# A fused Perceiver layer on one core: the cross-attention scores as plain fp32 matmuls in two column halves, and the order of three engines around them

## What is computed

```python
q = query @ Wq.T + bq;  k = mem_state @ Wk.T + bk;  v = mem_state @ Wv.T + bv
scores = jnp.einsum('btd,bsd->bts', q, k) * scale
vals, idx = jax.lax.top_k(scores, 32)          # all others are -inf
attn = jax.nn.softmax(masked, axis=-1)
x1 = x + jnp.einsum('bts,bsd->btd', attn, v) @ Wo.T + bo
```

## Time and profile before

| | us |
|---|---|
| median of 3 runs (lowest, highest) | 459.78 (457.98, 460.98) |
| the profiled execution | 461.32 |
| its span in the trace | 459.5 |
| TensorE busy | 439.7 (96%) |
| VectorE busy | 299.3 (65%) |
| ScalarE busy | 215.7 (47%) |
| GpSimd busy | 127.2 (28%) |

### The profile page before, as it was taken

The page is one execution under the profiler, slowest core; times in us unless marked ns, Lnnn a source line. Parts: engine busy times, 40 slices in busy tenths (PEclk is TensorE's granted clock), DMA queues, the critical chain, the costliest instruction groups (busy, mean ns, idle before and its releaser), DMA issues.

```text
span 459.5 us, 5828 instructions
## 1 busy us (share of the span) xinstructions
PE 439.7 (96%) x2045; PEld 325.5 (71%) x2045; DVE 299.3 (65%) x591; ACT 215.7 (47%) x321; POOL 127.2 (28%) x195
## 2 busy tenths in 40 slices
PE   6999999799999999898999999999999999999996
PEld 2587766356567656576888888887788888888884
DVE  3898787688999999968997443646862333522224
ACT  1797764354566454384877446434542111111111
POOL 3501013032222330200003272324236643333330
PEclk9999999799999999999999999999999999999999
DMA  6999924044224314103951700000000000200002
GB/s 207 412 391 386 366 98 180 2 183 183 74 112 183 139 45 184 35 11 141 396 198 38 168 1 23 1 0 1 1 1 1 1 0 1 86 7 0 1 0 92
DMA packets 26845, 49.98 MB, mean 109 GB/s; under 512 B 6208, under 2 KB 6208, under 8 KB 25792
## 3 DMA queue, kind: packets, MB, share of 16 engines
q1 hardware_dynamic: 26816, 49.61, 30.2%
HBM read 47.49 MB, written 2.11 MB: 108 GB/s over the span
## 4 chain that ended last, share of the span: by engine, by line
PE 71%; DVE 13%; ACT 6%; DMA 5%; issue 3%; SPq 1%; POOL 0%; DVEq 0%; ACTq 0%
PE bank L1237 8%; PE bank L1239 8%; PE bank L1238 8%; PE bank L1447 7%; PE bank L1678 7%; PE bank L1676 6%; PE bank L1662 6%; PE bank L1663 6%; PE bank L1418 5%; PE bank L1344 3%; DMA wab<-w1T 2%; PE bank L1244 2%; DVE mt_lo L1026 2%; PE bank L1432 2%; DVE work L1039 2%
## 5 line engine op out<-in xcount | busy, mean ns | idle before, releaser
L792 ACT ACTIVATE g<-bank,b1c 128x512 f32<-128x512 f32 x32 | 22.0, 688 | 92.0 <-PE bank L1678 92.0
L1217 DVE CAST g_hi<-g 128x512 fp32r<-128x512 f32 x32 | 13.9, 436 | 74.7 <-ACT g L792 74.6
L594 ACT ACTIVATE mt_hi<-bank 128x512 fp32r<-128x512 f32 x64 | 38.0, 600 | 49.4 <-PE bank L1418 49.4
L1026 DVE TENSOR_TENSOR mt_lo<-bank,mt_hi 128x512 fp32r<-128x512 f32 x64 | 43.1, 684 | 18.1 <-ACT mt_hi L594 17.9
L1676 PE MATMUL bank<-xt_lo,w1s 128*128 128x512 f32 x128 | 50.8, 397 | 0.0
L1678 PE MATMUL bank<-xt_hi,w1s 128*128 128x512 f32 x128 | 50.7, 396 | 0.0
L1662 PE MATMUL bank<-w2s,g_lo 128*128 128x512 f32 x128 | 50.3, 393 | 0.2 <-DVE g_lo L1219 0.2
L1663 PE MATMUL bank<-w2s,g_hi 128*128 128x512 f32 x128 | 50.0, 390 | 0.0
L487 POOL TENSOR_SCALAR w2s<-w2t 128x512 fp32r<-128x512 int8 x32 | 19.8, 620 | 65.9 <-PE bank L1663 65.9
L445 POOL TENSOR_SCALAR qs<-qT 128x256 fp32r<-128x256 f32 x16 | 6.5, 405 | 112.8 <-PE bank L1433 93.5
L1432 PE MATMUL bank<-mt_lo,qs 128*128 128x512 f32 x64 | 30.6, 479 | 0.3 <-DVE mt_lo L1026 0.3
(11 more groups left out here) (244 smaller groups left out, 1101.0 us busy)
## 6 DMA issues: line engine op xcount, KB each, us to landing
ctxr<-ctx SPq DMA_DIRECT2D x8, 1024.0 KB, 8.5
ctx<-ctx SPq DMA_DIRECT2D x8, 1024.0 KB, 7.7
wab<-w1T SPq DMA_DIRECT2D x4, 1024.0 KB, 11.4
wab<-w2T SPq DMA_DIRECT2D x4, 1024.0 KB, 8.5
wgraw<-wgT SPq DMA_DIRECT2D x4, 1024.0 KB, 6.5
wst<-w1T SPq DMA_DIRECT2D x4, 1024.0 KB, 6.2
wst<-w2T SPq DMA_DIRECT2D x4, 1024.0 KB, 6.6
resid<-x SPq DMA_DIRECT2D x4, 512.0 KB, 6.8
```

What stands on the lines that cost most here:

```text
L594: act.activation(mt_hi[:, g % 4, :], ctx_bank(g)[:, :], ACT.Copy).then_inc(mt_hi_ok, 1)
L1026: dve.tensor_tensor(mt_lo[:, g % 4, :], ctx_bank(g)[:, :], f(mt_hi[:, g % 4, :]), ALU.subtract).then_inc(mt_lo_ok, 1)
```

## The change

Scores are plain fp32 matmuls like `weigh`: step `s` of four per pair takes chunk `d` of both batches, one in each column half, with `qT` itself as weights (64 columns) and the copied chunk `mt` as the moving operand; no split of context or queries is made. Chunks alternate between the two batches and always turn over two PSUM banks. One ScalarE activation with the bias `ctok` brings a pair's scores to `s_t` (`scores_part`). `wvo` is made wholly in iterations 0 and 1 in banks 6 and 7. `project(i - 2)` runs whole at the end of iteration `i`, so the statistics and the layer-norm turn of a pair come an iteration sooner, and the ninth iteration is gone. The tail is ordered anew on all engines; the weights' slots in `wgraw`, and where the split parts lie, change with it. `wst` has three slots instead of four, and `bias_o` is loaded earlier. GpSimd adds `bias_x` to all token tiles at once and then only does `rstd`.

The core of the diff; the lines removed from the old loops, which stand above, are left out, those of the tail are shown:

```diff
--- before.py
+++ after.py
...
-                if k < 4:
-                    sp.wait_ge(wg_lo_ok[w_slot(k)], DC)
+                if k < 3:
+                    sp.wait_ge(wg_lo_ok[k + 1], DC)
                 else:
-                    sp.wait_ge(tern_ok, k - 3)
+                    sp.wait_ge(tern_ok, k - 2)
...
+            def mt_part(g):
+
+                act.wait_ge(ctx_turned, g + 1)
+                if g >= 4:
+                    act.wait_ge(scored, g // 2 - 1)
+                act.activation(mt[:, g % 4, :], bank[g % 2][:, :], ACT.Copy).then_inc(mt_ok, 1)
+
+            def scores_part(p):
+
+                act.wait_ge(scored, DC * (p + 1))
+                if p:
+                    act.wait_ge(exp_ok, p)
+                    act.wait_ge(topk, 8 * p - 6)
+                else:
+                    act.wait_ge(ctok_ok, 1)
+                act.activation(s_t[:, :], bank[2 + p % 2][:, :], ACT.Identity, bias=ctok[:, p:p + 1],
+                               scale=1.0).then_inc(scores_ok, 1)
+
...
+            for i in range(NT):
+                g = 2 * DC * i
+                mt_part(g)
+                if i >= 1:
+                    scores_part(i - 1)
+                if i == 1:
+                    wvo_hi_part(1)
+                mt_part(g + 1)
                 if i == 2:
                     wvo_hi_part(3)
+                if i >= 1:
+                    keep_exp(i - 1)
+                mt_part(g + 2)
+                if i >= 3:
+                    ln2_apply(i - 3)
+                mt_part(g + 3)
                 if i == 0:
                     abs_part(7)
+                if i >= 2:
+                    am_part(i - 2)
+                mt_part(g + 4)
+                if i < 2:
+                    wvo_hi_part(2 * i)
+                mt_part(g + 5)
+                if i >= 3:
+                    xt_part(NT + i - 3, i - 3, ln2_bank(i - 3))
+                if i >= 2:
+                    amt_hi_part(i - 2)
+                mt_part(g + 6)
                 if i == NT - 1:
+                    split_hi(0, wk_hi, 0, DC // 2)
+                mt_part(g + 7)
+                if i == NT - 1:
+                    split_hi(0, wk_hi, DC // 2, DC)
+                if i >= 1:
+                    at_part(i - 1)
+
+            scores_part(7)
+            keep_exp(7)
             ln2_apply(5)
-            split_hi(1, wv_hi, 0, DC)
-            xt_part(NT + 4, 4, ln2_bank(4))
+            am_part(6)
             xt_part(NT + 5, 5, ln2_bank(5))
-            act.wait_ge(mt_used, 4 * B)
+            amt_hi_part(6)
+            split_hi(1, wv_hi, 0, DC // 2)
+            at_part(7)
+            split_hi(1, wv_hi, DC // 2, DC)
+            ln2_apply(6)
+            am_part(7)
+            amt_hi_part(7)
+            xt_part(NT + 6, 6, ln2_bank(6))
+            act.wait_ge(scored, DC * NT)
             split_hi(2, wgq_hi, 0, DC)
-            ln2_apply(6)
-            act.wait_ge(qs_ok, 4 * NT)
+            ln2_apply(7)
+            xt_part(NT + 7, 7, ln2_bank(7))
             split_hi(3, wgg_hi, 0, DC)
-            ln2_apply(7)
-            xt_part(NT + 6, 6, ln2_bank(6))
-            xt_part(NT + 7, 7, ln2_bank(7))
 
...
+            for i in range(NT):
+                if i >= 3:
+                    add_att(i - 3)
+                    ln2_stats(i - 3)
+                if i == 0:
+                    wvo_lo_part(0)
                 if i == 1:
+                    wvo_lo_part(1)
                     scales()
                 if i == 2:
                     wvo_lo_part(3)
+                if i >= 1:
+                    top8(i - 1, 0)
+                    top8(i - 1, 1)
                 if i == 1:
+                    wvo_lo_part(2)
+                if i >= 1:
+                    top8(i - 1, 2)
+                    top8(i - 1, 3)
+                    kept_part(i - 1)
                 if i >= 3:
+                    xt_lo_part(NT + i - 3, i - 3, ln2_bank(i - 3))
+                if i >= 2:
                     amt_lo_part(i - 2)
-            ln2_stats(4)
+                if i >= 1:
+                    rinv_part(i - 1)
+
+            split_lo(0, wk_lo, wk_hi)
+            add_att(5)
             ln2_stats(5)
+            top8(7, 0)
+            top8(7, 1)
+            xt_lo_part(NT + 5, 5, ln2_bank(5))
+            top8(7, 2)
+            top8(7, 3)
+            amt_lo_part(6)
+            kept_part(7)
+            rinv_part(7)
             dve.wait_ge(am_ps, NT - 1)
-            split_lo(0, wk_lo, wk_hi)
+            split_lo(1, wv_lo, wv_hi, 0, DC // 2)
             add_att(6)
-            amt_lo_part(NT - 1)
             ln2_stats(6)
-            xt_lo_part(NT + 4, 4, ln2_bank(4))
-            xt_lo_part(NT + 5, 5, ln2_bank(5))
+            split_lo(1, wv_lo, wv_hi, DC // 2, DC)
+            amt_lo_part(7)
+            xt_lo_part(NT + 6, 6, ln2_bank(6))
             dve.wait_ge(am_ps, NT)
-            split_lo(1, wv_lo, wv_hi)
-            split_lo(2, wgq_lo, wgq_hi)
             add_att(7)
             ln2_stats(7)
+            split_lo(2, wgq_lo, wgq_hi)
 
             dve.wait_ge(kvb_in, 32)
             dve.wait_ge(att_ps, NT)
...
                 else:
-                    xt_lo_part(NT + 6, 6, ln2_bank(6))
+                    xt_lo_part(NT + 7, 7, ln2_bank(7))
                     split_lo(3, wgg_lo, wgg_hi)
-                    xt_lo_part(NT + 7, 7, ln2_bank(7))
                 dve.wait_ge(v_ps, t + 1)
...
                         pe.wait_ge(wv_in, 16)
-                        pe.wait_ge(norm_ok, 1)
+                        pe.wait_ge(mix_ok, 1)
                     elif d == 1:
-                        pe.wait_ge(lag_ok, 2)
-                        pe.wait_ge(scale_ok, 1)
+                        pe.wait_ge(xbias_ok, 1)
                     else:
...
+            def k_product(t, ds):
+
+                if ds[0] == 0:
+                    pe.wait_ge(xt_lo_ok, NT + t + 1)
+                    if t >= 2:
+                        pe.wait_ge(kb_ok, t - 1)
+                for d in ds:
                     if t == 0:
...
+            def chunk(i, j):
+
+                g, b, d = 2 * DC * i + j, 2 * i + j % 2, j // 2
+                if d == 0:
+                    pe.wait_ge(ctx_in[b % 8], 16 * (b // 8 + 1))
+                if g < 2:
+                    pe.wait_ge(q_ok, g + 5)
+                else:
...
+            def score(s):
+
+                pair, d = s // DC, s % DC
+                pe.wait_ge(mt_ok, 2 * s + 2)
+                if d == 0:
+                    if pair < 2:
+                        pe.wait_ge(q_ok, 7 + pair)
+                    else:
+                        pe.wait_ge(scores_ok, pair - 1)
+                for par in range(2):
+                    b = 2 * pair + par
+                    ins = pe.matmul(bank[2 + pair % 2][par * T:par * T + T, :], qT[:, d, b * T:b * T + T],
+                                    mt[:, (2 * s + par) % 4, :], start=(d == 0), stop=(d == DC - 1))
+                ins.then_inc(scored, 1)
+
...
+            for i in range(NT):
+                s0 = DC * i
+                chunk(i, 0)
+                if i:
+                    score(s0 - 1)
+                if i == 1:
+                    totals()
+                chunk(i, 1)
+                if i < 2:
+                    wvo_step(2 * i, (0, 1))
+                else:
+                    weigh(i - 2, (0, 1))
+                chunk(i, 2)
+                score(s0)
+                chunk(i, 3)
+                if i < 2:
+                    wvo_step(2 * i, (2, 3))
+                else:
+                    weigh(i - 2, (2, 3))
+                chunk(i, 4)
+                score(s0 + 1)
+                chunk(i, 5)
+                if i < 2:
+                    wvo_step(2 * i + 1, (0, 1))
+                if i >= 3:
+                    ln2_turn(i - 3)
+                if i >= 2:
                     join(i - 2)
+                chunk(i, 6)
+                score(s0 + 2)
+                chunk(i, 7)
+                if i < 2:
+                    wvo_step(2 * i + 1, (2, 3))
+                if i >= 1:
                     turn_prob(i - 1)
+                if i >= 2:
+                    project(i - 2)
+
+            score(DC * NT - 1)
+            weigh(6, (0, 1, 2, 3))
+            k_product(0, (0, 1))
+            join(6)
+            k_product(0, (2, 3))
+            ln2_turn(5)
+            project(6)
+            turn_prob(7)
+            k_product(1, (0, 1))
             weigh(7, (0, 1, 2, 3))
+            k_product(1, (2, 3))
             join(7)
-            k_product(0)
-            ln2_turn(4)
-            ln2_turn(5)
-            project(7, (0, 1, 2, 3))
-            k_product(1)
             ln2_turn(6)
             v_product(0)
+            project(7)
+            k_product(2, (0, 1, 2, 3))
+            v_product(1)
             ln2_turn(7)
-            v_product(1)
-            for t in range(2, NT):
-                k_product(t)
-                v_product(t)
+            for t in range(3, NT):
```

(54 more changed lines are left out.)

463 lines of the change are left out of this document (98 added, 365 removed).

## The result

The changed kernel takes 477.62 us (median of 4 runs, 476.68 to 478.45) against 459.03 us for the kernel before (4 runs, 457.98 to 460.98): ratio 1.040, 95% interval 1.036 to 1.044. The forecast was 478.0. The profiled execution took 477.32 us against 461.32, that is +16.0, where the prediction's sum had +18.2.

A forecast was written before the change was run, and what follows sets the result against it. TensorE was taken to set the pace, VectorE close behind. Terms 7.0 - 12.2 - 2.9 + 17.6 + 8.7 = +18.2 us on the profiled 461.32 gave 479.5, less 1.5 for the median: 478.0 us, range 466 to 483.

The forecast's parts named there:

- scores: Cross attention: 32 half-width score steps of 1.16 us replace 64 chunk scores of 0.47, +7.0 us on TensorE.
- eleven waits gone: TensorE's eleven waits between 80 and 249 us all vanish, -12.2 us.
- clock behind the `wvo_lo` wait: Half-clock stretch from 85.70 to 91.50 us, behind the wait ahead of the first `weigh`, goes: -2.9 us.
- three waits of the tail: New TensorE waits at `project(6)`, `k_product(2)` and `k_product(3)`: 5.0, 5.0 and 7.6 us, together +17.6 us.
- three clock falls: Granted clock falls to half behind each of the three new tail waits, 2.9 us each, +8.7 us.
- the halves do not overlap: Rival on score steps: one matmul in each half does not overlap, step 2.03 us, total 506; chance 0.03.
- the entry is much cheaper: Rival on score steps: entry between transposes far below 0.30 us, -9.6 at the most, 468.4; chance 0.07.
- The other side: Rival, not slower: all 48 score and weighing groups lose their entry, -14.4 us, 463.6 with three falls; chance 0.06.
- the clock holds in some of the waits: Rival on the tail: two clock falls give 475.1, one 472.2, none 469.3 us; chance 0.22.
- The first part and everything else unchanged: Work from the first `wgq` matmul on stays; work leaving VectorE, ScalarE and GpSimd counts only through waits it causes.
- From the profiled time to the median: Last step of the sum: the median taken as 1.5 us below the profiled execution, 479.5 to 478.0 us.

The follow-up runs named there:

- t123_all_waits: The changed kernel with TensorE, VectorE and ScalarE reordered in the tail so that all three tail waits go: 452.44 us, ratio 0.988 to the kernel before.

## Why the prediction was right, and where it was not

Its terms, against the profiled runs:

| term | predicted | measured |
|---|---|---|
| scores | +7.0 | a step 1.16 as predicted; all of TensorE's own work +5.1 |
| eleven waits gone | -12.2 | none is left; the pair is 16.23 |
| clock behind the `wvo_lo` wait | -2.9 | -2.96 profiled, -1.1 in the median |
| three waits of the tail | +17.6 | +18.5 |
| three clock falls | +8.7 | +6.1 profiled, 7.3 in the median |
| GpSimd beside VectorE, `habs` | not seen | +2.2 |

The +5.1 is a difference. From the first chunk to the first `wgq` matmul it is 198.29 us before (from 50.34) and 212.36 now (from 52.46); without waits (by starts 12.2 for the eleven and 0.5 for a short one at 52 us, now 18.5) and cold clock (2.9, now 6.1) 182.6 and 187.8 remain. With 12.2 and 2.9 for the second and third, the terms give 5.1 - 12.2 - 2.9 + 18.5 + 6.1 + 2.2 = +16.8, less the 0.5 of the short wait +16.3, where +16.0 was measured. A check by another trace is t123_all_waits: 5.1 - 12.2 - 2.9 - 0.5, and 1.1 and 0.6 for the two waits left in it, give -8.8 us; its profiled run is 8.8 us under that of before. No run tests the -12.2 by itself.

- **The mechanism was right.** Scores cost TensorE more than before, all waits of the pairs go for it, and the tail's order gives back more than that. The runs show the tail's part by itself: take its waits away and the sign turns (452.44 us), keep them and only hold the clock, and 7.3 us go.
- **The scores.** The step was priced right, 1.16 us with an entry of 0.30: two chunks with and without a step between them give it, each doubled step costs 0.86, and grouping gains 0.30 us a group. What was too high is the +7.0 as TensorE's whole additional work: by starts chunks and scores take 6.4 us more (0.3 of the difference is the last score, which stands beside the weighing of pair 6), `wvo` and the weighing are unchanged, the turns take 0.7 and the projections 0.8 us less, k and v 0.3 more. The prediction had the projection as only moved; what makes it and the turns shorter no run isolates. The rivals "the halves do not overlap" and "the entry is much cheaper" are out. "The other side" too: the entry is there behind transposes.
- **The three waits.** By starts, less what the work ahead takes (0.36 for a turn, 0.23 for a matmul), they are 192.47 - 186.96 = 5.5, 5.2 net; 215.78 - 210.14 = 5.6, 5.4 net; 231.52 - 223.28 = 8.2, 7.9 net. The prediction had 5.0, 5.0, 7.6; the hand-overs, which I put at nothing or 0.1 us, and the rounding of the steps make some 0.3 us each. Which engine, which tile and what is queued in front were as it said, in all three.
- **The clock** was the term that was mis-sized most: +8.7, taken as three times the one example of the earlier trace rows: +6.1 in the profiled run, 7.3 in the median. A fall costs 1.7 to 2.9 us, and no wait showed more than the example, the longest neither. The rival "the clock holds in some of the waits" did not come: behind each wait of 4.9 us or more the clock was at half, in all six traces in which such waits stand.
- **"The first part and everything else unchanged"** was wrong in one place. I priced what leaves GpSimd as worth nothing, and did not look at what then starts sooner on it. The eight additions run in one block from 45.34 us, beside VectorE steps on TensorE's path: 2.2 us. It is the step that failed. The page SBUF — State Buffer of the Trainium skill, in SBUF: two separate sides, says that a VectorE instruction with two SBUF inputs and a GpSimd instruction that reads SBUF lock each other out. The rows agree: the steps with two SBUF inputs lose 0.7 to 1.1 us, under the 1.25 us of one addition, and the sums that read PSUM beside them stay at 0.68. Small steps with one input lose as well: `tensor_scalar` on `rnorm` takes 0.77 us instead of 0.17 and on `ctok` 1.01 instead of 0.23, neither on TensorE's path here.
- **From the profiled time to the median** I took off 1.5 us, as for the kernel before. That was a second mistake, and it met the others half-way. The profiled run of before was dear by a fall that half of its runs lack, while the profiled run of the changed kernel was a cheap one (477.32 against a median of 477.62, with the cheapest three falls of four such traces). By profiled runs the sum was 2.2 us too high (479.5 against 477.32); by the median it came within 0.4 us. Part of that closeness is luck.

What stays open: why the clock falls in some runs behind a wait of 2.0 or 2.8 us and not in others, and why the cold stretch behind one and the same wait lasts 3.5 us in one run and 5.3 in another. No run here controls it.

## What to carry to other kernels

When a change takes work off the engines that are not the pace, ask of each what it will now run sooner and beside whom, and go through the order of the tail by hand, where the pipeline's slack is gone: here 25 us of waits and cold clock stood in three places, and another order of the same instructions there turned 4% slower into 1% faster. Work in column halves pays its entry for each group, so put such groups side by side. And before a time is taken from one profiled run, see whether its granted clock is that of the other runs.
